# Moving one expert's weight transfers from before the gathers to behind them

## Chip, cores and metric
The kernel runs on one core of one Trainium2 chip. The metric is the time of one execution on the device in microseconds (us); the figure given for a kernel is the median of its runs.

## What is computed
The reference is one block of cross attention with a mixture of experts behind it, all in float32:

```python
x = x + xattn(layernorm(x), ctx, Wq, bq, Wk, bk)       # x: 4 x 256 x 256, ctx: 4 x 256 x 128
# the experts, on tokens = layernorm(x) as 1024 rows of 256; E = 8, capacity C = 160
logits = tokens @ gate_weight.T
probs, top1 = softmax(logits), argmax(logits)
mask = one_hot(top1, E); ranks = cumsum(mask, axis=0) - 1; mask = mask * (ranks < C)
combine = (mask * probs)[:, :, None] * one_hot(rank of the token, C)[:, None, :]
dispatch = einsum('tec,th->ech', combine != 0, tokens)
hmid = gelu(einsum('ech,ehi->eci', dispatch, wi))       # wi: 8 x 256 x 1024
eout = einsum('eci,eih->ech', hmid, wo)                 # wo: 8 x 1024 x 256
x = x + einsum('tec,ech->th', combine, eout)
```

Each token goes to one expert, and each expert takes at most 160 tokens, by rank.

## The kernel before
The attention comes first (to about 30 us). Its result, 1024 rows, is kept in `rows` together with each row's mean, reciprocal deviation, index and weight (260 numbers, 1040 bytes a row). POOL scatters the rows by eight indirect DMAs (`scatter`, line 339) into `slots_dram`, a table in DRAM of 8 experts by 160 slots; all of them together raise `scattered` to 16 * NT. The table has been filled with defaults by a DMA earlier. The first expert's activations are built in another way, by matmuls with one-hot matrices (`disp`), so that `mm1(0)` needs no gather.

SP issues nearly all other transfers, in an order written out by hand, and one SP queue carries them: inputs, the fill of the table, then by `weights(e)` (lines 223 to 225) two transfers of 1 MB for each expert, `wi_sb[:, e]` and `wo_sb[:, e]`. After the wait for `scattered` (line 249) follow the gathers: `got[:, 1]`, `got[:, 0]`, `got[:, 2:E]` (the first 128 slots of the experts), `rest[:, 1]` (slots 128 to 159 of experts 4 to 7; ACT issues `rest[:, 0]` at line 491). Then four transfers `out_v[b] <- rows` write the attention's result to the output (`x1_out`), two transfers `last_slots(r)` (lines 227 to 231) fetch the slots from 128 on once more in another layout, and then come `weights(3)` to `weights(7)`.

TensorE (PE) works in program order. For each expert, `mm1(e)` multiplies the slots by `wi` (32 matmul instructions, waits for `wi_here[e]`), ACT applies the gelu into `gelu`, and `mm2(e, n)` multiplies by `wo` (16 instructions, waits for `wo_here[e]`). `dT(i)` (line 967) transposes a tile of gathered slots that DVE has normalised into `stok` (`load_tile`, line 746), and DVE copies it to `dispT` (`load_tileT`). The order is mm1(0), mm2(0) with dT(0) and dT(1) inside it, mm1(1) with dT(2) inside it, dT(3), mm1(2), mm2(1), dT(4), dT(5), mm1(3), mm2(2), dT(6), mm1(4), mm2(3) and the remaining slots of experts 0 to 3 (`mm2_stack`), mm1(5) and so on. `mm` is a helper, so most matmuls have its line, 822, and transposes have line 819. So dT(0) and dT(1) need `got_one` and `rest_here[0]`, dT(2) and dT(3) need `got_main`.

POOL adds the experts' results by indirect DMAs from `y` into the output rows (line 370, `out_tile` on DVE makes them); the first of these waits for `x1_out` to reach 16 * B, since it writes to the same rows. `y` has two buffers, so that `out_tile(2)` waits for the first of them to have landed.

Of the kernel before, what the change touches and what calls it, by code (L numbers as in the profile page):

```python
# [61 lines left out]
def xattn_moe(nc, x_in_v, xT_v, head_v, wi_v, wo_v, out):  # L62
# [5 lines left out]
    with ExitStack() as stack:  # L68
# [141 lines left out]
        @block.sync  # L210
        def _(sp):
            def head(i):
                a, z = HEAD[i]
                sp.dma_start(small[:, a:z], head_v[:, a:z]).then_inc(head_here[i], 16)  # L214

            def inputs(i):
                a, z = X_PARTS[i]
                sp.dma_start(x_sb[:, a:z, :], x_in_v[a // 4][:, a % 4:a % 4 + z - a, :]).then_inc(x_here[i], 16)  # L218

            def turned_inputs(i):  # L220
                sp.dma_start(xT[:, 2 * i:2 * i + 2, :, :], xT_v[i]).then_inc(xT_here[i], 16)

            def weights(e):
                sp.dma_start(wi_sb[:, e, :, :], wi_v[e]).then_inc(wi_here[e], 16)
                sp.dma_start(wo_sb[:, e, :, :], wo_v[e]).then_inc(wo_here[e], 16)

            def last_slots(r):
                first = r * PER_STACK
                sp.dma_start(got[:, E + r, :],
                             by_rank[P:CAP, first:first + PER_STACK, :].rearrange("q j w -> j q w")  # L230
                             ).then_inc(got_rem[r], 16)

            head(0)
            head(1)
            inputs(0)
            inputs(1)
            head(2)
            turned_inputs(0)
            inputs(2)
            turned_inputs(1)  # L240

            sp.wait_ge(fill_done, 2)
            sp.dma_start(slots_dram.rearrange("(n p) r -> p n r", p=P),
                         fill[:, None, :].to_broadcast([P, E * CAP // P, ROW])).then_inc(filled, 16)
            weights(0)
            weights(1)
            weights(2)

            sp.wait_ge(scattered, 16 * NT)
            sp.dma_start(got[:, 1, :], by_rank[0:P, 1, :]).then_inc(got_one, 16)  # L250
            sp.dma_start(got[:, 0, :], by_rank[0:P, 0, :]).then_inc(got_zero, 16)
            sp.dma_start(got[:, 2:E, :], by_rank[0:P, 2:E, :]).then_inc(got_main, 16)
            sp.dma_start(rest[:, 1, :], by_rank[P:CAP, PER_STACK:E, :]).then_inc(rest_here[1], 16)
            for b in range(B):
                sp.dma_start(out_v[b], rows[:, 2 * b:2 * b + 2, 0:H]).then_inc(x1_out, 16)
            last_slots(0)
            last_slots(1)
            for e in range(3, E):
                weights(e)
# [828 lines left out]
```

## Time and profile before

| | |
|---|---|
| median of 3 runs | 109.61 us (109.61 to 110.08) |
| the profiled execution | 110.13 us, of which the span is 108.3 us |
| PE busy | 101.4 us (94%) |
| PE weight loads busy | 89.9 us (83%) |
| DVE, ACT, POOL busy | 33.2, 33.0, 31.0 us |
| moved by DMA | 25.76 MB, mean 238 GB/s |
| mean granted clock of TensorE | 0.988 of full |

The span is what the trace shows, from the first instruction to the last; the 1.8 us around it belong to the execution too. "SPq" lines of the trace are DMA issues on SP; "us to landing" counts from the start of the issue to the moment when the transfer is complete.

### The profile page before, as it was taken

How to read it: one execution, taken by the hardware profiler on the slowest of the kernel's cores; microseconds unless marked ns; L12 is line 12 of the kernel's file. 1: busy time of each engine (PE TensorE's matmuls, PEld its weight loads, DVE VectorE, ACT ScalarE, POOL GpSimd, SP SyncE). 2: the span in 40 equal slices, each digit the busy share in tenths (PEclk: the TensorE clock that was granted, in tenths of full speed). 3: DMA queues.
4: the chain of work that ended last, by engine and by line, in shares of the span. 5: the costliest groups of instructions: out<-in, count | busy, mean ns of one | idle time of the engine just before them, and what ended most of it. 6: DMA issues, size and time to landing. Idle time of an engine off the chain costs nothing.

```text
span 108.3 us, 1960 instructions
## 1 busy us (share of the span) xinstructions
PE 101.4 (94%) x744; PEld 89.9 (83%) x744; DVE 33.2 (31%) x135; ACT 33.0 (30%) x87; POOL 31.0 (29%) x58
## 2 busy tenths in 40 slices
PE   5999999989999989999999999999999999999910
PEld 5875987869999779998998998669989999988900
DVE  0055898999710143600510400220020010011210
ACT  4139678865651302341041041002302303200000
POOL 5710599677770000030200200303003003012550
PEclk9999999999999999999999999999999999999995
DMA  2989999999992879999999999960001001001100
GB/s 74 273 298 355 355 321 408 424 412 420 415 387 100 176 235 377 332 316 396 436 421 415 421 430 414 424 244 33 0 0 42 0 6 48 0 0 47 54 3 3
DMA packets 7713, 25.76 MB, mean 238 GB/s; under 512 B 912, under 2 KB 4245, under 8 KB 5656
## 3 DMA queue, kind: packets, MB, share of 16 engines
q1 hardware_dynamic: 6680, 23.39, 58.2%
q0 software_dynamic: 880, 2.12, 5.3%
q10 hardware_dynamic: 144, 0.13, 0.5%
q8 instruction: 6, 0.10, 0.3%
q14 instruction: 3, 0.02, 0.1%
HBM read 21.14 MB, written 4.76 MB: 239 GB/s over the span
## 4 chain that ended last, share of the span: by engine, by line
PE 75%; DMA 12%; POOL 3%; issue 2%; DVE 2%; SPq 2%; ACT 0%; ACTq 0%
PE ps L822 68%; DMA shared<-in_head 5%; PE ps L866 4%; DMA slots_dram<-rows,slot 4%; DMA rest<-slots_dram 3%; POOL slots_dram L339 2%; PE ps L819 2%; POOL out L377 1%; DVE rows L561 1%; SPq L218 1%; SPq L214 1%; DVE stats L619 0%; DVE stok L746 0%; ACT attended L388 0%; DVE y_end L798 0%
## 5 line engine op out<-in xcount | busy, mean ns | idle before, releaser
L822 PE MATMUL ps<-wo_sb,shared 128*32 128x128 f32 (+2 forms) x320 | 36.4, 337 | 0.0
L822 PE MATMUL ps<-shared,wi_sb 128*128 128x160 f32 x244 | 34.6, 299 | 0.0
L822 PEld LDWEIGHTS ps<-shared,wi_sb 128*128 128x128 f32 x244 | 33.6, 190 | 0.1
L822 PEld LDWEIGHTS ps<-wo_sb,shared 128*32 128x32 f32 (+1 forms) x320 | 29.2, 142 | 5.0 <-issue 0.7
L493 ACT ACTIVATE shared<-ps 128x480 f32<-128x480 f32 (+1 forms) x24 | 12.5, 526 | 48.9 <-PE ps L822 48.4
L370 POOL DMA_INDIRECT out<-y,got x9 | 8.8, 974 | 60.8 <-DVE y L780 44.1
L780 DVE SCALAR_TENSOR_TENSOR y<-ps,share,got 128x256 f32<-128x256 f32 x9 | 4.4, 484 | 48.1 <-PE ps L822 24.7
L822 PE MATMUL ps<-shared 128*128 128x256 f32 (+1 forms) x28 | 9.5, 481 | 0.1
L339 POOL DMA_INDIRECT slots_dram<-rows,slot x8 | 8.2, 1021 | 3.4 <-DVE slot L604 1.9
L822 PE MATMUL ps<-attended,shared 128*128 128x272 f32 x32 | 8.3, 398 | 0.5 <-ACT attended L388 0.5
L822 PEld LDWEIGHTS ps<-shared 128*128 128x128 f32 x28 | 6.0, 229 | 2.2 <-issue 1.0
L822 PEld LDWEIGHTS ps<-attended,shared 128*128 128x128 f32 x32 | 5.8, 190 | 1.6 <-ACT attended L388 0.6
L746 DVE TENSOR_SCALAR stok<-got 128x256 f32<-128x256 f32 x7 | 2.7, 415 | 9.8 <-DMA got<-slots_dram 9.8
L866 PE MATMUL ps<-turner,shared 128*128 128x136 f32 x32 | 4.9, 287 | 0.0
L919 PE MATMUL ps<-shared 128*128 128x160 f32 (+1 forms) x32 | 4.9, 304 | 0.0
L866 PEld LDWEIGHTS ps<-turner,shared 128*128 128x128 f32 x32 | 4.3, 189 | 0.5 <-ACT turner L421 0.2
L919 PEld LDWEIGHTS ps<-shared 128*128 128x128 f32 x32 | 4.4, 190 | 0.2
L520 DVE BATCH_NORM_STATS2 stats<-shared 128x6 f32<-128x256 f32 x8 | 3.1, 415 | 4.7 <-DMA shared<-in_x 4.7
L323 POOL TENSOR_SCALAR shared<-shared,shift 128x256 f32<-128x256 f32 x8 | 4.0, 512 | 1.4 <-DVE shift L533 1.3
L826 PE MATMUL ps<-warm_w 128*128 128x128 f32 x12 | 2.9, 410 | 1.1 <-DVE warm_w L498 1.1
L561 DVE SCALAR_TENSOR_TENSOR rows<-ps,rstd,shared 128x256 f32<-128x256 f32 x8 | 3.8, 474 | 0.3 <-PE ps L822 0.2
L406 ACT ACTIVATE shared<-ps,nmax 128x256 f32<-128x256 f32 x8 | 3.7, 472 | 0.3 <-DVE nmax L538 0.3
(87 smaller groups left out, 72.3 us busy)
## 6 DMA issues: line engine op xcount, KB each, us to landing
wi_sb<-in_wi SPq DMA_DIRECT2D x8, 1024.0 KB, 15.6
wo_sb<-in_wo SPq DMA_DIRECT2D x8, 1024.0 KB, 18.9
slots_dram<-fill SPq DMA_DIRECT2D x1, 1300.0 KB, 12.6
shared<-in_xT SPq DMA_DIRECT2D x2, 512.0 KB, 7.3
out<-rows SPq DMA_DIRECT2D x4, 256.0 KB, 5.6
got<-slots_dram SPq DMA_DIRECT2D x1, 780.0 KB, 6.3
got<-slots_dram SPq DMA_DIRECT2D x4, 130.0 KB, 2.5
shared<-in_x SPq DMA_DIRECT2D x2, 256.0 KB, 4.0
```

What stands on the lines that cost most here:

```text
L323: nc.gpsimd.tensor_scalar(x_sb[:, n, :], x_sb[:, n, :], 1.0, shift1[:, n:n + 1], ALU.mult, ALU.add).then_inc(xs_done, 1)
L339: nc.gpsimd.indirect_dma_start(slots_dram, bass.IndirectOffsetOnAxis(ap=slot[:, n:n + 1], axis=0), rows[:, n, :], None, bounds_check=last_ ...
L370: nc.gpsimd.indirect_dma_start(out_rows, bass.IndirectOffsetOnAxis(ap=got[:, t, INDEX:INDEX + 1].bitcast(I32), axis=0), y[:, n % 2, :], No ...
L406: nc.scalar.activation(att[:, b, m, :], p_en[b][:, m * S:(m + 1) * S], ACT.Exp, bias=nmax[:, n:n + 1], accum_out=esum[:, n:n + 1]).then_in ...
L493: nc.scalar.activation(gelu[:, e % RING, a:z, :], p_h[j][:, 0:(z - a) * CAP], ACT.Gelu).then_inc(gelu_done, 1)
L520: nc.vector.bn_stats(stats[:, 0, n, 0:6], x_sb[:, n, :]).then_inc(bn1_done, 1)
L561: nc.vector.scalar_tensor_tensor(halves(rows[:, n, 0:H]), halves(p_xm[n // 2 % 2][:, n % 2, 0:WIDE])[:, :, E:HALF], rstd1[:, n:n + 1], hal ...
L780: nc.vector.scalar_tensor_tensor(y[:, n % 2, :], p_o[n % 2][:, 0:H], share[:, t:t + 1], got[:, t, 0:H], ALU.mult, ALU.add).then_inc(y_done, 1)
L822: return nc.tensor.matmul(dst, lhsT, rhs, start=(k == 0), stop=last)
L826: nc.tensor.matmul(p_warm[:, 0:P], warm_w[:], warm_w[:], start=True, stop=True)
L866: last = nc.tensor.matmul(p_at[c][:, E + m * P:E + m * P + HALF], att[:, b, m, c * P:(c + 1) * P], turner[:, b % 2, m * HALF:(m + 1) * HAL ...
L919: last = nc.tensor.matmul(p_disp[c][:, 0:width], tok[:, n, c * P:(c + 1) * P], onehot[:, n, 0:width], start=(n == 1), stop=(n == NT - 1), ...
```

## The change

`weights(2)` is issued behind the gathers and ahead of the rows' output, instead of behind `weights(1)` and ahead of the wait for `scattered`. Its two transfers, 1 MB each, are the same. All else stays, in order and in content.

```diff
@@ -242,15 +242,16 @@
             sp.wait_ge(fill_done, 2)
             sp.dma_start(slots_dram.rearrange("(n p) r -> p n r", p=P),
                          fill[:, None, :].to_broadcast([P, E * CAP // P, ROW])).then_inc(filled, 16)
+
             weights(0)
             weights(1)
-            weights(2)
 
             sp.wait_ge(scattered, 16 * NT)
             sp.dma_start(got[:, 1, :], by_rank[0:P, 1, :]).then_inc(got_one, 16)
             sp.dma_start(got[:, 0, :], by_rank[0:P, 0, :]).then_inc(got_zero, 16)
             sp.dma_start(got[:, 2:E, :], by_rank[0:P, 2:E, :]).then_inc(got_main, 16)
             sp.dma_start(rest[:, 1, :], by_rank[P:CAP, PER_STACK:E, :]).then_inc(rest_here[1], 16)
+            weights(2)
             for b in range(B):
                 sp.dma_start(out_v[b], rows[:, 2 * b:2 * b + 2, 0:H]).then_inc(x1_out, 16)
             last_slots(0)
```

## Rows read from the trace of the kernel before

**Rows 1.** The page's part 2: 40 slices of 2.7 us.

```profile
PE   5999999989999989999999999999999999999910
DMA  2989999999992879999999999960001001001100
```

**Rows 2.** Timeline of PE: start, us, line, tiles; merged runs of instructions.

```profile
34.97 2.95 PE L822 MATMUL ps<-wo_sb,shared 128*128 128x256 f32 x12
38.58 0.44 PE L819 MATMUL ps<-idg,stok 128*128 128x128 f32 x2 [0.35 <-DVE stok L746]
39.73 3.42 PE L822 MATMUL ps<-shared,wi_sb 128*128 128x160 f32 x24
42.98 0.38 PE L819 MATMUL ps<-idg,stok 128*128 128x128 f32 x2
44.51 4.51 PE L822 MATMUL ps<-shared,wi_sb 128*128 128x160 f32 x32
48.86 3.62 PE L822 MATMUL ps<-wo_sb,shared 128*128 128x256 f32 x16
52.31 0.60 PE L819 MATMUL ps<-idg,stok 128*128 128x128 f32 x4
52.75 4.51 PE L822 MATMUL ps<-shared,wi_sb 128*128 128x160 f32 x32
60.77 4.51 PE L822 MATMUL ps<-shared,wi_sb 128*128 128x160 f32 x32
```

**Rows 3.** The chain of work that ended last: start, us, what.

```profile
31.08 4.03 DMA slots_dram<-rows,slot
35.14 2.95 DMA rest<-slots_dram
```

**Rows 4.** Timeline of SP's issues: start, us, line.

```profile
36.47 0.62 SPq L253 DMA_DIRECT2D rest<-slots_dram  x1
42.09 0.84 SPq L224 DMA_DIRECT2D wi_sb<-in_wi  x1
42.98 0.43 SPq L225 DMA_DIRECT2D wo_sb<-in_wo  x1
43.45 1.16 SPq L224 DMA_DIRECT2D wi_sb<-in_wi  x1
48.12 2.31 SPq L225 DMA_DIRECT2D wo_sb<-in_wo  x1
```

**Rows 5.** DMA issues in windows at 37.9, 42.1, 42.9, 43.5, 49.0, in that order; last column landing.

```profile
rest<-slots_dram SPq DMA_DIRECT2D x1, 130.0 KB, 6.2
wi_sb<-in_wi SPq DMA_DIRECT2D x1, 1024.0 KB, 9.9
wo_sb<-in_wo SPq DMA_DIRECT2D x1, 1024.0 KB, 11.5
wi_sb<-in_wi SPq DMA_DIRECT2D x1, 1024.0 KB, 13.5
wo_sb<-in_wo SPq DMA_DIRECT2D x1, 1024.0 KB, 27.3
```

**Rows 6.** POOL's indirect DMAs, windows at 53.3, 81.4, 102.5: us to landing.

```profile
out<-y,got POOLq DMA_INDIRECT x1, 7.4
out<-y,got POOLq DMA_INDIRECT x1, 2.4
out<-y_end,half_index POOLq DMA_INDIRECT x1, 2.6
```

**Rows 7.** Timeline of POOL and DVE: the first write of y, the third y.

```profile
46.26 0.97 POOL L370 DMA_INDIRECT out<-y,got  x1 [14.20 <-DMA out<-rows]
60.81 0.48 DVE L780 SCALAR_TENSOR_TENSOR y<-ps,share,got 128x256 f32<-128x256 f32 x1 [6.27 <-issue]
```

**Rows 8.** Stretches: us, busy (count) of five engines, granted clock, DMA share, GB/s.

```profile
103.50:104.00 0.50, 0.00 (x0) 0.00 (x0) 0.32 (x1) 0.00 (x0) 0.00 (x0) 1.00 0.00 0
105.60:105.80 0.20, 0.00 (x0) 0.00 (x0) 0.00 (x0) 0.00 (x0) 0.00 (x0) 0.90 0.16 35
105.80:106.00 0.20, 0.00 (x0) 0.00 (x0) 0.00 (x0) 0.00 (x0) 0.00 (x0) 0.50 0.03 0
```

**Rows 9.** Tile ps: ns min/median/max, first and last start; then PE's timeline.

```profile
L826 PEld LDWEIGHTS ps<-warm_w x12: 190/333/333, 1.1 to 30.2; 128*128 128x128 f32 x12
L990 PEld LDWEIGHTS ps<-shared,wi_sb x12: 186/190/190, 30.5 to 32.0; 128*128 128x128 f32 x12
3.93 1.49 PE L822 MATMUL ps<-shared 128*128 128x256 f32 x3
6.49 0.99 PEld L822 LDWEIGHTS ps<-shared 128*128 128x128 f32 x4
```

## The prediction
> **What bounds the kernel now.** I read the slices of busy time first: PE stands at nine tenths in nearly all of them from the second slice to the last but two, while DMA is full up to slice 26 and nearly empty after it, apart from a dip in slice 12 [rows 1]. PE is the bound, and the transfers matter only where one arrives after PE wants it. So the second view is PE's timeline against the landings. PE goes from expert to expert without a gap once the first transposes are through: mm1(1) at 39.73, mm1(2) at 44.51, mm2(1) at 48.86, mm1(3) at 52.75, mm1(4) at 60.77 [rows 2]. The one place ahead of that where PE waits for data is the second transpose of mm2(0), at 38.58. Its chain is the last scatter's landing (issued 31.08, 4.03 us), then the gather `rest<-slots_dram` (2.95 us), then DVE's stok [rows 3]. The third view is the list of SP's issues with their landings. Issue plus landing time gives wi of expert 3 at 42.09 + 9.9 = 52.0, wo of expert 3 at 42.98 + 11.5 = 54.5, wi of expert 4 at 43.45 + 13.5 = 56.95, wo of expert 7 at 48.12 + 27.3 = 75.4 [rows 4, 5]. Expert 3's wi is thus there just 0.75 us before mm1(3) starts at 52.75, and expert 4's has 3.8 us to spare. That 0.75 us is the number on which this change turns. The spacing from wi(3) to wo(3) and on to wi(4) is 2.5 us a megabyte, which I take as the price of a weight transfer on the slowest of the DMA engines.
>
> **Part one, what is taken from ahead of the gathers.** Two transfers of 1 MB leave the stretch before 35 us. They stood behind weights(1), so weights(0) and weights(1) land as before. The queue should be dry about 4.9 us earlier, so before the last scatters are issued. What those gain: the last scatter landed 4.03 us after its issue at 31.08, beside the end of wo(2) [rows 3]. POOL's writes of y, of nearly the same size, took 7.4 us beside the weights and 2.4 us without, and the half-size ones 2.6 [rows 6]. With an empty queue I take 2.5, which brings `scattered` from 35.1 to 33.6: a gain of 1.5 us, bounds 0 (the 4.03 is POOL's and the memory's own latency) and 1.65 (2.4 us). POOL's and DVE's work that leads to the issue at 31.08 waits for no weights and stays. All gathers start earlier by that 1.5.
>
> For PE this is worth less than 1.5. With stok there in time, mm2(0) would run from 34.97 without gaps. Its rate is that of mm2(1), 16 instructions from 48.86 to 52.31, so 0.216 us each [rows 2]. 16 of them and two pairs of transposes at 0.22 a pair (four took 52.31 to 52.75) make 3.45 + 0.44 = 3.9, so mm1(1) would start at 38.9 and not at 39.73. PE gains at most 0.87 us, and it keeps this up to dT(2), for which got_main comes earlier too. mm1(2) would then start at 43.65 and mm1(3) at 51.9, if their weights were there.
>
> **Part two, what is put behind the gathers.** rest(1), the transfer ahead of the new place, landed at 36.47 + 6.2 = 42.7 [rows 4, 5], so 41.2 now. wi(2) then lands about 2.45 later, at 43.6, right when mm1(2) wants it (43.65): between no wait and 1.5 us if the scatters gain nothing. wo(2), at 46.1, is wanted 12 us later. On SP the two issues go ahead of the four outputs, the two last_slots and all later weights; each costs about 0.5 to 0.9 us of SP's time [rows 4], which is hidden since the queue behind them is deep. What isn't hidden is the work of the DMA engines: everything behind the new place shifts by 2 x 2.45 = 4.9 us, less the 1.5 that the gathers started earlier, so by 3.4 us. x1_out moves from 46.2 to 49.6, and with it the first write of y on POOL (46.26). Even with 7.4 us to landing this is done by 57, ahead of the third y on DVE at 60.81 [rows 6, 7]; nothing else on POOL or DVE is late through it. The last_slots are wanted only at 69. But wi(3) moves from 52.0 to 55.4, and mm1(3) is ready at 51.9. **PE stands still for 3.5 us**, and after that the work is as before: wo(3) at 57.9, wi(4) at 60.3, all ahead of their uses, which shift as well.
>
> **The sum.** mm1(3) starts at 55.4 plus under 0.1 for the restart, against 52.75: +2.7 us. Note that PE's earlier gain of 0.87 and a possible wait of mm1(2) do not enter, since wi(3) alone sets this start. Written out: 52.0 - 52.75 + 4.9 - 1.5 + 0.05 = +2.7. With the scatter gain at its bounds it is +2.55 to +4.2. The profiled execution of 110.13 would become 112.8 (span 108.3 to 111.0); it lies 0.5 above the median of 109.61, so the median becomes 112.3.
>
> How sure is the lag of wi(3)? Behind rows of 1 KB the engines may lose less than before if large weight packets fill their pauses. 1.3 MB of gathers, 1 MB of output, 0.26 MB of last_slots and 1 MB of wi(3) took from 36 to 52 us, 3.6 MB in 16 us or 225 GB/s, where the weights alone run at some 420. I keep 1.5 us of room below for this.
>
> The Trainium skill bears on one piece of that lag (DMA: Bandwidth & Descriptors, section on why a DMA increments its semaphore by 16): the number of DMA engines on which a transfer runs is the largest up to 16 that divides the slowest dimension of both sides. For last_slots that dimension is 4, so four engines would carry all its rows and be late for wi(3). The trace agrees as far as it goes: wo(7) lands at 75.4 while the DMA slices fall from full to nearly nothing at about 72 [rows 1, 4, 5]. By this rule the lag stays where it is, in full, behind weights(2) too.
>
> **Rival A: the clock of TensorE falls in the new gap.** In this trace the granted clock is at its upper level (2.4 GHz) until about 105.7 and reads 0.50 (1.2 GHz) from then on; PE does nothing any more from 103.5, so it fell 2.2 us into the idleness [rows 8]. The gap of 3.5 us is longer than that; against it speaks that the last work there was of small matmuls, and that where in a gap the clock falls may differ from run to run. How long slow work then lasts can be bounded from the start: the warm-up's weight loads have a median of 333 ns, and those of mm1(0) 190; 256-column matmuls stand 0.43 apart (3 from 3.93) where later they stand 0.216; the loads are at full rate from about 6.5 on [rows 9]. So slow work lasted some 5.3 us from the first matmul at 1.1. Half of such a stretch is lost: 2.6 us, and as its end is seen once only I allow a third to either side, 1.7 to 3.5. The time would be 112.3 + 2.6 = 114.9 us. The page TensorE: Matmul & The Clock Gate of the Trainium skill (Part 1) names this mechanism: a wait of PE for a DMA drops the clock and the next matmuls start cold. By it this case is the outcome whenever the gap is long enough.
>
> **Rival B: faster.** Here the scatters gain their 1.5, PE its 0.87, and wi(3) is in time since the slow stretch from 36 to 46 us was a loss of pauses, not of engine time, which weights(2) now fills. The point where this decides: wi(3) must land by 51.9, so 3.5 us earlier than in my sum. It gives 109.61 - 0.87 = 108.75. For it speaks that 225 GB/s is far below the rate of the weights; against it that the DMA slices read 8, 7, 9 tenths busy there already [rows 1].
>
> **Rival C: no change.** The shift and the hiding nearly cancel: wi(3) lands between 52.2 and 53.2, and mm1(3) starts where it started. 109.6.
>
> **How the numbers follow.** The plain stall (sum, 112.3; by its bounds 110.8 to 113.8) 0.48. Rival A (114.9; 113.5 to 117) 0.37. Rival B 0.08, rival C 0.07. Range: from 110.7, the plain stall with all the room given to the engines' pauses, to 115.8, which takes in most of rival A. The plain stall and A together are the slower side, 0.85; a measurement of this kernel can tell about 0.5% from no change, 0.55 us, and the sum is five times that.
>
> **What would show it.** In the changed kernel: the last scatter lands by 33.6 and the gathers are issued there; PE reaches mm1(1) near 38.9; x1_out is near 49.6; wi(3) lands near 55.4, and the matmuls of expert 3 carry an idle time of 3 to 4 us with the DMA of wi_sb as its releaser; experts 4 to 7 show none. Rival A would show 0.5 in the granted clock behind the gap and matmuls of twice the spacing. The prediction is wrong if wi(3) lands by 52, or if mm1(2) waits for wi(2) by more than 1.5 us, since then the slow engines are slower behind the gathers than I assume.

## The result

The changed kernel took 114.2 us (median of 4 runs, 112.50 to 115.38) against 109.84 for the kernel before in the same comparison (109.61 to 110.32). The ratio is 1.030, 95% interval 1.017 to 1.043: it is slower. Every ratio in this document leaves out the executions that are more than 1.5% above the fastest of their kernel, here the two longest of the four; the medians alone stand at 1.040. The profiled execution is one of 115.38 us with a span of 113.6.

The page's part 2, now in slices of 2.84 us (PE, the granted clock of TensorE, DMA), to be read beside [rows 1]:

```profile
PE   6979999989999999993199999999999999999920
PEclk9999999999999999999959999999999999999995
DMA  3799999994228999999999999951000101001100
```

Counted from 1, PE has a hole in the slices 19 and 20, at 51 to 57 us, and right behind it the clock has one at half. DMA shows the other side: its dip, one slice long before, now begins at 26 us and lasts into the gathers, while its full stretch ends later.

The timeline of PE (start, us, line, tiles) beside [rows 2]:

```profile
34.95 2.75 PE L823 MATMUL ps<-wo_sb,shared 128*128 128x256 f32 x12
37.54 0.60 PE L820 MATMUL ps<-idg,stok 128*128 128x128 f32 x4
38.84 3.42 PE L823 MATMUL ps<-shared,wi_sb 128*128 128x160 f32 x24
43.62 4.51 PE L823 MATMUL ps<-shared,wi_sb 128*128 128x160 f32 x32
51.43 0.60 PE L820 MATMUL ps<-idg,stok 128*128 128x128 f32 x4
56.23 6.29 PE L823 MATMUL ps<-shared,wi_sb 128*128 128x160 f32 x32 [4.21 <-DMA wi_sb<-in_wi]
62.36 3.62 PE L823 MATMUL ps<-wo_sb,shared 128*128 128x256 f32 x16
66.03 4.51 PE L823 MATMUL ps<-shared,wi_sb 128*128 128x160 f32 x32
```

Up to the transposes at 51.43 PE is 0.88 us ahead of the kernel before: mm2(0) has no gap, and mm1(1) starts at 38.84 instead of 39.73. Then it stands still for 4.21 us until wi of expert 3 is there. mm1(3) starts at 56.23 where it started at 52.75: +3.5. And mm1(3) itself takes 6.29 us instead of 4.51: +1.8. From there on all is as before, and mm1(4) stands at 66.03 instead of 60.77: +5.3 us, which is the whole difference of the two spans (113.6 - 108.3).

Where the two extra transfers went is in the chain of work that ended last (start, us, what), beside [rows 3]:

```profile
31.05 2.44 DMA slots_dram<-rows,slot
33.51 0.33 SPq L250
35.52 0.58 SPq L224
41.81 14.38 DMA wi_sb<-in_wi
56.23 9.74 PE ps L823 x48
```

The last scatter lands 2.44 us after its issue instead of 4.03; the gathers are issued at 33.51 instead of 35.13. But the chain no longer runs through a gather to the transposes: it goes down SP's queue to wi(3), issued at 41.81 and there at 56.2. The other landings, from issue plus time to landing: wi(2) 42.4, wo(2) 45.95, the outputs 49.5, wo(3) 46.36 + 12.4 = 58.8.

The clock behind the gap, in stretches (us, busy and count of PE, weight loads, DVE, ACT, POOL, granted clock, DMA share, GB/s):

```profile
55.50:56.00 0.50, 0.00 (x0) 0.00 (x0) 0.00 (x0) 0.00 (x0) 0.00 (x0) 1.00 1.05 442
56.40:56.60 0.20, 0.20 (x2) 0.20 (x3) 0.00 (x0) 0.00 (x0) 0.00 (x0) 0.71 1.23 512
56.50:57.00 0.50, 0.50 (x4) 0.50 (x4) 0.00 (x0) 0.00 (x0) 0.00 (x0) 0.50 1.02 426
59.00:59.50 0.50, 0.50 (x4) 0.50 (x3) 0.00 (x0) 0.00 (x0) 0.00 (x0) 0.50 0.79 328
59.80:60.00 0.20, 0.20 (x3) 0.20 (x2) 0.00 (x0) 0.20 (x1) 0.00 (x0) 0.76 1.17 492
60.00:60.50 0.50, 0.50 (x6) 0.50 (x5) 0.00 (x0) 0.20 (x1) 0.00 (x0) 1.00 0.98 410
```

It falls to the lower level (1.2 GHz) at about 56.5, some 0.25 us after the matmuls have begun again, and is back at the upper one (2.4 GHz) at about 59.9: some 3.4 us of work at half rate, which costs half of it, 1.7, near the 1.8 that mm1(3) is longer.

### The profile page after: what moved, and what is told of

Same layout as the page of the kernel before. It is cut to its first block, busy times and chain, and to the rows that moved or that the text cites. A ratio compares the mean times of both kernels' runs of the same rounds, so it can differ in the third digit from the quotient of the medians.

```text
span 113.6 us, 1960 instructions
## 1 busy us (share of the span) xinstructions
PE 102.2 (90%) x744; PEld 91.0 (80%) x744; DVE 33.1 (29%) x135; ACT 33.2 (29%) x87; POOL 30.9 (27%) x58
## 4 chain that ended last, share of the span: by engine, by line
PE 60%; DMA 20%; SPq 8%; POOL 3%; issue 3%; DVE 2%; ACT 0%; ACTq 0%
PE ps L823 55%; DMA wi_sb<-in_wi 13%; DMA shared<-in_head 5%; PE ps L867 4%; POOL slots_dram L340 2%; SPq L256 2%; DMA slots_dram<-rows,slot 2%; SPq L229 2%; POOL out L378 1%; DVE rows L562 1%; SPq L218 1%; PE ps L820 1%; SPq L214 1%; SPq L253 1%; SPq L224 1%
## 5 line engine op out<-in xcount | busy, mean ns | idle before, releaser
L823 PE MATMUL ps<-shared,wi_sb 128*128 128x160 f32 x244 | 36.4, 309 | 4.2 <-DMA wi_sb<-in_wi 4.2
L823 PEld LDWEIGHTS ps<-shared,wi_sb 128*128 128x128 f32 x244 | 35.2, 198 | 4.6 <-DMA wi_sb<-in_wi 4.4
L823 PEld LDWEIGHTS ps<-shared 128*128 128x128 f32 x28 | 5.4, 208 | 2.9 <-issue 1.3
L920 PEld LDWEIGHTS ps<-shared 128*128 128x128 f32 x32 | 4.4, 190 | 0.2
L754 DVE COPY shared<-ps 128x256 f32<-128x256 f32 x7 | 2.9, 419 | 3.3 <-PE ps L820 3.3
```

The costliest lines, as they stand in the source:

```text
L754: nc.vector.tensor_copy(dispT[:, :, t, 0:P], p_dT[i % 2][:, 0:H].rearrange("p (c s) -> p c s", c=HC)).then_inc(dT_sb, 1)
L823: return nc.tensor.matmul(dst, lhsT, rhs, start=(k == 0), stop=last)
L920: last = nc.tensor.matmul(p_disp[c][:, 0:width], tok[:, n, c * P:(c + 1) * P], onehot[:, n, 0:width], start=(n == 1), stop=(n == NT - 1), ...
```

## Experiments

Each kernel ran beside the kernel before on its chip. e1, e2, e4 and e6 shared one chip; the seven others ran on another, in two groups. The comparison of each is with the kernel before in its own group: 111.06 us for the first four, 110.04 for e3, e5, e7, e8, and 110.18 for e9, e10, e11.

### The changed kernel again (e1, e10)

No edit.

> The changed kernel once more, for the spread of its times. My theory is that each execution has the same stall of about 4.2 us ahead of mm1(3), and that they differ by whether TensorE's clock falls at its end. In the profiled execution the matmuls of expert 3 took 6.29 us instead of 4.51, so a fall costs 1.8 us. Then the times come in two groups 1.5 to 3 us apart, and the mean granted clock goes with them: 0.974 in the longer ones (113.9 to 115.4 us so far), 0.989 in the shorter (112.5). The rival is that the spread comes from where wi(3) lands, with the clock as a bystander: then the times spread evenly from 112.5 to 115.4, and the mean clock says nothing of them.

> The changed kernel once more, to stand beside the short filler on one chip. So far the mean clock was 0.972 to 0.975 in four executions of it (113.9 to 115.4 us) and 0.986 to 1.000 in six (112.2 to 114.1). Expected: again two kinds, the first of them 1.5 to 2 us longer than the second on average; where wi(3) lands differs by some 1.5 us from run to run besides, so that single times of the two kinds may overlap.

All sixteen executions of the changed kernel, with the mean granted clock of each, in the order in which they ran:

| | us (mean clock) |
|---|---|
| first comparison | 115.38 (0.974), 114.47 (0.974), 112.50 (0.989), 113.94 (0.974) |
| e1, before: 111.06 | 114.11 (0.999), 113.21 (0.986), 112.68 (0.990), 112.24 (0.991), 114.89 (0.972), 113.28 (1.000) |
| e10, before: 110.18 | 113.88 (0.972), 112.50 (1.000), 115.15 (0.964), 111.89 (0.992), 114.40 (0.975), 114.20 (0.979) |

The kernel before never shows a mean clock under 0.986 in the 62 executions of the three groups (a fall at the very end of the kernel, as in [rows 8], is all that its two traces show). The changed kernel has eight executions under 0.98, at 113.9 to 115.4 us, and eight above, at 111.9 to 114.1. Eight is the least number of falls behind the gap: 3.4 us at half rate takes only 0.015 from the mean, so that an execution at 0.986 (113.21 us in e1) can have either that fall or the one at the end. The median is 113.24 for e1 (1.020 of the kernel before; the ratio is 1.016, 1.012 to 1.019) and 114.04 for e10 (1.035; the ratio is 1.018, 1.012 to 1.024). So both statements of the expectation hold in part: the clock does split the times, by some 2 us in e10, and besides the place where wi(3) lands moves them. The trace of e1 shows a gap without a fall, that of e10 one with it:

```profile
55.83 4.61 PE L823 MATMUL ps<-shared,wi_sb 128*128 128x160 f32 x32 [2.94 <-DMA wi_sb<-in_wi]
```

```profile
54.91 6.18 PE L823 MATMUL ps<-shared,wi_sb 128*128 128x160 f32 x32 [3.26 <-DMA wi_sb<-in_wi]
```

The gaps differ by 0.3 us, the matmuls behind them by 1.57. In e10 the clock fell at about 54.7, 3.1 us after PE's last work and ahead of the matmuls, and was back at about 58.15. mm1(3) started, at the landing of wi(3), 22.7 us behind the issue of the first gather in the first trace, 21.9 in e1 and 21.7 in e10. What decides whether an execution has the fall is open, since the gaps of the untraced ones aren't known.

### Idle matmuls in the gap (e2, e9)

```diff
                 for i in INS_AT[s]:
                     dT(i)
+                if s == 3:
+                    keep_warm(16)
                 if s < E:
```

> The changed kernel with 16 idle matmuls of 128x128 put between dT(5) and mm1(3), so that PE works on zeros for most of the wait for wi(3). At full clock a pair of transposes of this size takes 0.22 us, so 16 take 3.5 us, less than the gap of 4.2, and mm1(3) can't start later for them. If the clock's fall costs 1.8 us of its own, the granted clock stays at 1.00 behind the gap, and all runs are near 112.5 us, 1.5 to 2 us under the longer group of the kernel without them. If the fall is a bystander, the time stays where it was, about 114.2.

Measured: 114.61 us (114.27 to 115.22, 6 runs), ratio 1.032 (1.029 to 1.035), longer than e1's 113.24. My expectation missed, and the timeline says why:

```profile
52.26 0.60 PE L820 MATMUL ps<-idg,stok 128*128 128x128 f32 x4
52.70 3.74 PE L827 MATMUL ps<-warm_w 128*128 128x128 f32 x32
56.27 4.51 PE L823 MATMUL ps<-shared,wi_sb 128*128 128x160 f32 x32
```

mm1(3) starts right behind the filler, with no idle time. The filler of 3.57 us was sized by the gap of the first trace; here the filler itself set the start. The trace has no landing for wi(3), but wi(4) landed at 60.7, and as it lands 5.1 to 5.4 us behind wi(3) in the traces of the changed kernel, wi(3) was there at about 55.4, by this estimate 0.9 us ahead of mm1(3). That it was so in the untraced executions too is not shown. That it kept the clock up (0.989 to 0.999 in all six, mm1(3) in 4.51 us) was hidden by what it cost. So e9 has half of it:

```diff
+                if s == 3:
+                    keep_warm(8)
```

> The changed kernel with 8 idle matmuls of 128x128 (1.8 us) ahead of mm1(3), where e2 had 16 (3.57 us). e2 kept the clock up in all six executions, but mm1(3) started right behind its filler, so that the filler itself set the start in most of them. 1.8 us is less than any gap that the changed kernel's times imply, and leaves at most 2.4 us idle. Theory: no execution has a mean clock under 0.98, and the longest times fall away: a range of 112 to 113.5 us where the kernel before is at 109.6 to 110, and a median 0.3 to 1.5 us under that of the changed kernel, by how many of its executions lose the clock. If the fall doesn't cost anything of its own, the two have the same median.

Measured: 112.25 us (111.91 to 113.89, 6 runs), against 114.04 for the changed kernel beside it (e10). All six have a mean clock of 0.989 or more. The trace:

```profile
51.41 1.95 PE L827 MATMUL ps<-warm_w 128*128 128x128 f32 x16
54.75 4.61 PE L823 MATMUL ps<-shared,wi_sb 128*128 128x160 f32 x32 [1.40 <-DMA wi_sb<-in_wi]
```

mm1(3) starts within 0.2 us of where it does in e10 (54.91), so the stall is the same; its matmuls take 4.61 us instead of 6.18. The medians differ by 1.8 us, and the two executions of e10 that kept their clock, at 112.50 and 111.89 us, are level with e9. The fall of the clock is a cost of its own, and work on zeros during the wait takes it away: none of the twelve executions of e2 and e9 has a mean clock under 0.989. One execution of 113.89 at 0.993 is longer than I expected of this kernel.

### The first half alone (e6)

Against the kernel before, as an extract; the lines that let the matmuls of expert 2 read the weights of expert 1, and wait for those, are left out here:

```diff
-            weights(2)
```

The result of this kernel is another, since it leaves out expert 2's weights.

> weights(2) is left out altogether; the matmuls of expert 2 read expert 1's weights instead, so its part of the result is another. This is the change's first half alone. My theory: the last scatter lands at 33.5 as in the changed kernel, mm2(0) runs without a gap, PE is 0.87 us earlier from mm1(1) to the end, and nothing is late: 108.7 to 108.9 us. Rival: the gain ahead of the gathers is lost again behind them (wi(3) at 52.0 had only 0.75 us to spare, and if it doesn't come earlier by the 1.6 us of the scatters it takes part of it back): 109.3 to 109.7.

Measured: 111.20 us (10 runs), ratio 1.0009 (0.9993 to 1.0025): no gain. mm2(0) ran without a gap and no matmul waited for a weight, as I said. But PE was late ahead of all this:

```profile
29.75 1.33 PE L919 MATMUL ps<-shared 128*128 128x160 f32 x8 [0.64 <-issue]
31.95 1.87 PE L990 MATMUL ps<-shared,wi_sb 128*128 128x160 f32 x12 [0.65 <-DVE shared L731]
40.26 3.42 PE L822 MATMUL ps<-shared,wi_sb 128*128 128x160 f32 x24
```

mm1(0) starts at 31.95 instead of 30.55, and so mm1(1) at 40.26, behind even the 39.73 of [rows 2]. On this chip DVE did `pick(6)` and the copy to dispT late, with nothing in the trace that held it. Where PE arrives at mm2(0) 1.4 us late, the gathers of the kernel before are in time for it, and an earlier scatter wins nothing. This would explain both the 111.06 of the kernel before on this chip and the missing gain, but the kernel before was not traced there, so it is argued, not shown. Nor does this run say what the first half alone would win on the other chip.

### The kernel before, traced beside others (e8)

No edit; it shared its chip with e3, e5 and e7.

> The kernel before, unchanged, traced on the same chip as the runs beside it. Where the chip was another (the runs of e1 to e6), the kernel before took 111.1 us and not 109.6, and the kernel without weights(2) won nothing, though its mm2(0) had no gap: there DVE started pick(6) some 0.9 us late and PE reached mm1(0) at 31.9 instead of 30.5. Theory: on such a chip PE is late at mm2(0) in the kernel before too (31.4 to 32 for mm1(0)), so the gathers are in time for it, and the 0.87 us that an earlier scatter can win are not there. Rival: the late start belongs to kernels without weights(2) ahead of the gathers, and here mm1(0) starts at 30.5 and mm2(0) has its gap of 0.3 to 0.8 us.

Measured: 110.45 us against 110.04 for the same kernel in its role as the one before, ratio 1.005 (1.001 to 1.009). The kernels are the same, so a difference of 0.5% between two of these kernels says nothing here, whatever its interval. mm1(0) starts at 30.48, and mm2(0) has its gap, so my theory on late chips could not be tested here. The trace also shows how tight the transfers are in the kernel before:

```profile
43.34 0.44 PE L819 MATMUL ps<-idg,stok 128*128 128x128 f32 x2 [0.18 <-DVE stok L746]
53.16 4.51 PE L822 MATMUL ps<-shared,wi_sb 128*128 128x160 f32 x32
```

got_main landed at 42.85 and dT(2) waited for it; wi(3) landed at 42.01 + 11.0 = 53.0, 0.15 us ahead of mm1(3).

### Half of the shift (e5)

Against the changed kernel, as an extract; `wi(e)` and `wo(e)` are the two transfers of `weights(e)`, each by itself:

```diff
             weights(1)
+            wi(2)
...
-            weights(2)
+            wo(2)
```

> Half the change: wi(2) stays ahead of the gathers, wo(2) alone goes behind them. By the shift on the queue, wi(3) lands 2.45 us earlier than in the changed kernel, so at 53 to 53.8, against an arrival of PE at 52 to 53: a gap of 0 to 1.5 us, no fall of the clock, and a time 0 to 1.2 us above before. The rival, that weights(2) disturbs the transfers behind it by more than its bytes, would leave more than half of the loss: 1.5 us or more above before.

Measured: 109.72 us (10 runs; two of them 110.81 and 112.62, the latter with a mean clock of 0.975), ratio 0.997 (0.993 to 1.001): no difference. I had expected no fall of the clock, and by its mean of 0.975 one of the ten has it. The trace:

```profile
52.33 4.61 PE L830 MATMUL ps<-shared,wi_sb 128*128 128x160 f32 x32 [0.99 <-DMA wi_sb<-in_wi]
```

wi(3) lands at 39.08 + 13.2 = 52.3, which is 19.3 us behind the first gather, against 21.7 in e10: 2.4 us for the one megabyte less. The price of a weight transfer in the sum holds, within what single traces of one kernel differ by (21.7 to 22.7 us). The gap of 1.0 us costs about what the earlier scatter wins.

### What the last_slots cost (e4, e3)

```diff
             def last_slots(r):
                 first = r * PER_STACK
-                sp.dma_start(got[:, E + r, :],
-                             by_rank[P:CAP, first:first + PER_STACK, :].rearrange("q j w -> j q w")
-                             ).then_inc(got_rem[r], 16)
+                for j in range(PER_STACK):
+                    sp.dma_start(got[j * REM:(j + 1) * REM, E + r, :],
+                                 by_rank[P:CAP, first + j, :]).then_inc(got_rem[r], 16)
```

The two waits for `got_rem` on DVE are raised to 16 * PER_STACK with it.

> The changed kernel with each of the two last_slots transfers issued as four, one for each expert, with 32 slots as the outer dimension of both sides. Same rows, same bytes, same place. wi(3) landed 6.7 us behind the outputs in the changed kernel (49.5 to 56.2) and 5.8 before, where 1 MB of weights takes 2.5. Theory: the two last_slots run on few DMA engines and delay wi(3) there by some 3 us beyond their 0.26 MB. Spread over all engines they take 0.6 to 1 us, wi(3) lands by 53 to 54, the gap ahead of mm1(3) shrinks to 1 to 2 us, the clock stays up, and the time is 110 to 111 us. Rival: the lag comes from the outputs' small rows, or from SP's 4.5 us issue of wi(3); then wi(3) lands at 56 or, by the six more issues on SP, later, and the time is 114 or more.

Measured: 111.99 us (4 runs), ratio 1.010 (1.006 to 1.013), against 1.016 for the changed kernel on the same chip. That is 1 us more than I expected, on a chip where the kernel before takes 111.06. Issues in the windows of wi(4), in e1 and then in e4 (last column us to landing; issued at 46.53 and at 47.42):

```profile
wi_sb<-in_wi SPq DMA_DIRECT2D x1, 1024.0 KB, 14.6
```

```profile
wi_sb<-in_wi SPq DMA_DIRECT2D x1, 1024.0 KB, 10.9
```

And the start of mm1(3) on e4's timeline of PE:

```profile
53.39 4.51 PE L823 MATMUL ps<-shared,wi_sb 128*128 128x160 f32 x32
```

wi(4) lands at 58.3 instead of 61.1, though the gathers were issued at the same time (33.90 and 33.95), and mm1(3) starts at 53.39 without a wait in the traced execution. Eight transfers in place of two are faster by 2.8 us for what stands behind them. The first version of them moves 0.26 MB, and 0.26 MB at the weights' rate of 2.45 us a megabyte would be 0.6 us. This agrees with the rule of the Trainium skill that the prediction named (DMA: Bandwidth & Descriptors, on why a DMA increments its semaphore by 16), by which a transfer with an outer dimension of 4 runs on four engines and one of 32 on sixteen. How many engines carried a transfer no view here shows. The rival that SP's issues or the outputs are the cause is out: the eight issues took SP 6.47 us and wi(3) was issued 4 us later than in e1 (45.89 and 41.73), and it was there by 53.39 instead of 55.8, though the first write of y, which waits for the outputs, went out no earlier (50.41 and 49.97).

In e3 the two transfers are as they were, but behind weights(3):

```diff
+            weights(3)
             last_slots(0)
             last_slots(1)
-            for e in range(3, E):
+            for e in range(4, E):
```

> The changed kernel with both last_slots issued behind weights(3) instead of ahead of it. If they alone cost wi(3) some 3 to 4 us on few DMA engines, wi(3) lands about 3.5 us earlier, at 52 to 53, the gap ahead of mm1(3) is under 1 us, and the time is within 0.7 us of the kernel before (0 to +0.6%). If their cost were only that of their 0.26 MB, wi(3) would land 0.6 us earlier and the time would stay 1.5 to 4 us above before.

Measured: 109.85 us (10 runs), ratio 1.0005 (0.997 to 1.004). As expected: wi(3) lands at 38.63 + 12.3 = 50.9, 17.6 us behind the first gather instead of 21.7, so the last_slots cost it some 4 us. SP's issue of wi(3), its size and time to landing, and then PE, where mm1(3) doesn't wait but the expert behind it does:

```profile
38.63 1.86 SPq L224 DMA_DIRECT2D wi_sb<-in_wi  x1
wi_sb<-in_wi SPq DMA_DIRECT2D x1, 1024.0 KB, 12.3
```

```profile
51.37 4.51 PE L824 MATMUL ps<-shared,wi_sb 128*128 128x160 f32 x32
60.37 4.61 PE L824 MATMUL ps<-shared,wi_sb 128*128 128x160 f32 x32 [0.82 <-DMA wi_sb<-in_wi]
```

The same delay falls on wi(4) now, which had 3.8 us to spare in the kernel before, where wi(3) had 0.75.

### wi(3) ahead of the outputs and the last_slots behind weights(4) (e7, e11)

Against the changed kernel, as an extract; `wi(e)` and `wo(e)` are those of e5:

```diff
             weights(2)
+            wi(3)
             for b in range(B):
                 sp.dma_start(out_v[b], rows[:, 2 * b:2 * b + 2, 0:H]).then_inc(x1_out, 16)
+            wo(3)
+            weights(4)
             last_slots(0)
             last_slots(1)
-            for e in range(3, E):
+            for e in range(5, E):
```

> The changed kernel with wi(3) right behind weights(2), ahead of the outputs, and the last_slots behind weights(4). Theory: wi(3) lands at about 48.5, no matmul waits for a weight, nothing of the 3 us stall is left, and what the earlier scatter wins stays: 0.87 us under the kernel before where PE reaches mm1(0) at 30.5, and level with it where PE is late there. Rival: the outputs now land at about 52 instead of 49.5, the first write of y is out 2.5 us later, and DVE's third y, wanted at 60, waits for it, and mm2 behind it: level or 0.5 us slower.

> The kernel of e7 (wi(3) right behind weights(2), ahead of the outputs, last_slots behind weights(4)) on another chip. Expected 0.8 to 1.2 us under the kernel before where PE reaches mm1(0) at 30 to 30.5, that is where DVE's pick(6) isn't late; level with it otherwise.

Measured: 108.83 us (12 runs, 108.41 to 109.60), ratio 0.991 (0.988 to 0.994), and again 108.50 us (5 runs, 108.46 to 109.50), ratio 0.984 (0.980 to 0.988). Both ratios are beyond the 0.5% by which the same kernel differed from itself. e11 ran on the same chip as e7, not on another as its expectation says, and it won 1.7 us, more than the 0.8 to 1.2 expected. In the trace of e7, on PE:

```profile
38.35 3.42 PE L832 MATMUL ps<-shared,wi_sb 128*128 128x160 f32 x24
51.38 4.51 PE L832 MATMUL ps<-shared,wi_sb 128*128 128x160 f32 x32
59.40 4.51 PE L832 MATMUL ps<-shared,wi_sb 128*128 128x160 f32 x32
```

and on POOL:

```profile
51.72 0.97 POOL L380 DMA_INDIRECT out<-y,got  x1 [20.17 <-DVE y L790]
```

PE has no gap from mm1(0) to the end. wi(3) is there at 36.14 + 12.0 = 48.1. The first write of y is on its way at 51.7, 5.5 us later than in [rows 7], and the third y isn't held by it. So the change's own idea, to clear the queue for the scatters, does win once the transfer that had 0.75 us to spare is not pushed back by it. How much of the gain is its own is not separated: against the trace of e8, PE leads by 0.44 us at mm1(0) already (30.04 and 30.48), ahead of all gathers and without a cause that the traces show, and by 1.39 at mm1(1); and the kernel before was not run with the last_slots alone moved.

## Why the prediction was right, and where not

- **What bounds.** PE, and the 0.75 us of wi(3) as the number on which it turns: right. The wait of 4.21 us stands on this transfer and no other.
- **The scatter's gain.** 1.5 us forecast, 1.6 measured (4.03 to 2.44 us); the gathers at 33.6 forecast, 33.51 measured. PE's 0.87: measured 0.89 at mm1(1) in the traces of the first comparison. e6 won nothing, which I put down to PE's late arrival at mm2(0); that is argued, not shown.
- **wi(2).** Forecast to land at 43.6 with mm1(2) ready at 43.65; it landed at 42.4, and mm1(2) didn't wait. got_main landed at 39.56, 5.2 us after its issue instead of 6.3. In e9, with the same order of transfers, it took 6.1, and in e7 and e11, which share one order, 6.1 and 4.7, so the difference isn't explained by what follows the gathers.
- **The shift of wi(3).** The term 4.9 us for two weight transfers: e5 measured 2.4 for one. For the two together single traces give 4.0 to 5.8: wi(3) lands 17.7 us behind the first gather in e8 against 21.7 in e10 on the same chip, and 16.9 in the first trace of the kernel before against 22.7 in the changed one's. The outputs at 49.6 forecast, 49.5 measured. wi(3) at 55.4 forecast, 56.2 measured, since it came 6.7 us behind the outputs and not 5.8; in e1 the same pair is 5.9 us apart, so this term varies by about 1 us from one execution to another. The room of 1.5 us below, for pauses that large packets would fill, was needed at most for the 0.9 us by which e10 and e8 stay under 4.9.
- **The plain stall, 112.3 us.** The one execution of the first four in which the clock stayed up took 112.50. That is the case for which the sum was made. All three traces of the changed kernel show its mechanism, a wait for wi(3). The size holds by this one execution, which was not traced, and by the two of e10 that kept their clock, 1.7 and 2.3 us above the kernel before, against the 2.7 of the sum.
- **Which case is the usual one.** Here the prediction failed in part. It gave the plain stall 0.48 and the fall of the clock (rival A) 0.37; in the first comparison the fall came in three of four executions, so that the median, 114.2, is rival A's case. Over the sixteen executions it came in eight at least, so which of the two cases the first four would show was partly luck. The step that misled is the argument that the end of the kernel may not stand for a gap in its middle; gaps of 3.26 and 4.21 us brought a fall in the two traces that have them. The page TensorE: Matmul & The Clock Gate of the Trainium skill (Part 1), named there for this rival, says that a wait of PE for a DMA makes the next matmuls start cold. These two traces agree (mm1(3) in 6.29 and 6.18 us instead of 4.5 to 4.6), while the trace of e1 has a wait of 2.94 us without it.
- **The price of a fall.** 2.6 us by half of the slow stretch at the kernel's start, bounds 1.7 to 3.5. Measured 1.8 (6.29 against 4.51), 1.6 (6.18 against 4.61) and 1.8 by the medians of e9 and e10: at the lower bound. The term was too large since the start of the kernel, from which it was taken, needed 5.3 us to reach full rate, and behind the gap the clock was low for only 3.4 us, in the first trace as in e10.
- **The sum by these.** 52.0 - 52.75 + 4.9 - 1.6 + 0.9 (the later landing) + 1.8 gives +5.25, and the spans differ by 5.3.
- **Rivals B and C.** The weights did not fill the pauses of the slow stretch by anything near the 3.5 us that B needed, and the shift was far from cancelling. What gave B's time is another order: e7 has it.

## What to carry to other kernels

Before a transfer is moved back in a queue, list every transfer behind the new place with its landing and the moment when it is wanted: it is the one with the least to spare that pays, here one that the edit doesn't touch. Waits of PE of 3.3 and 4.2 us cost another 1.6 to 1.8 us here through the clock; eight idle matmuls (1.8 us), shorter than the wait, took that away, and sixteen (3.6 us) cost more than they saved. Look for transfers with a small outer dimension ahead of urgent ones: 0.26 MB of them delayed a weight by 4 us.

## What the runs showed of the hardware that I had not expected

- The clock: through a gap of 2.94 us it stayed at its upper level (e1); at gaps of 3.26 us (e10) and 4.21 us (the first trace) it fell, 3.1 and 4.5 us after PE's last work ahead of the gap, and was back after 3.4 us. At the end of the kernel before it fell after 2.2 us [rows 8]. In [rows 9] the work at the start of the kernel was at half rate for 5.3 us, while the trace's granted clock reads 1.00 there.
- The same kernel on the same chip (e10) ran with mean clocks from 0.964 to 1.000. Whether the executions without a fall had shorter gaps is open.
- Two transfers of 130 KB over an outer dimension of 4 hold up the queue by some 4 us (e3); as eight of 32.5 KB with 32 rows each, 2.8 us of that is gone (e4).
- One issue on SP took 4.5 us: that of wi(3), from 41.81 to 46.31, with the outputs ahead of it not yet landed. In e4 the same issue took 1.0 us, behind eight short ones.
- On one chip PE reached mm1(0) at 31.4 to 32.05 in four traces, in the nine other traces at 29.8 to 30.8, with the same instructions ahead of it. The cause is open.
